# Feed-forward blocks in rounds of eight instead of steps of four: transposes, second layer and first layer grouped, with one bank for the first layer

## The reference, cut to what matters

```python
def _fff(x, node_w, node_b, w1, b1, w2, b2):
    for _ in range(DEPTH):                       # 4 levels, 15 nodes
        score = einsum('nd,nd->n', xf, node_w[cur]) + node_b[cur]
        cur = 2 * cur + 1 + (score >= 0)
    leaf = cur - N_NODES                         # one of 16 leaves
    hidden = relu(xf @ w1[leaf] + b1[leaf])      # 256 -> 64
    return hidden @ w2[leaf] + b2[leaf]          # 64 -> 256
q, k, v = _fff(x, q...), _fff(x, k...), _fff(x, v...)
attn = softmax(einsum('bqd,bkd->bqk', q, k) / 16)
return einsum('bqk,bkd->bqd', attn, v)
```

## Time and profile before

| | |
|---|---|
| median of 3 runs | 696.19 us (692.74 to 698.44) |
| span of the profiled execution | 651.9 us |
| median above that span | 44.3 us |
| TensorE busy | 585.3 us, 90% |
| VectorE busy | 439.3 us, 67% |
| ScalarE busy | 298.7 us, 46% |
| GpSimd busy | 236.6 us, 36% |
| FFN stage: transposes | 288, first at 429.8 us |
| FFN stage: last second-layer product starts | 554.1 us |

### The profile page before, as it was taken

The page is one execution under the profiler, slowest core; times in us unless marked ns, Lnnn a source line. Parts: engine busy times, 40 slices in busy tenths (PEclk is TensorE's granted clock), DMA queues, the critical chain, the costliest instruction groups (busy, mean ns, idle before and its releaser), DMA issues.

```text
span 651.9 us, 14814 instructions
## 1 busy us (share of the span) xinstructions
PE 585.3 (90%) x5131; PEld 492.2 (76%) x5131; DVE 439.3 (67%) x1511; ACT 298.7 (46%) x482; POOL 236.6 (36%) x298
## 2 busy tenths in 40 slices
PE   6577998999899999999999898769999999399996
PEld 6466787887787788878878776658888888289985
DVE  3755676888886888898888887845545553056664
ACT  4104444444443444544445454027777777133231
POOL 5700010053243243324323335740017777346431
PEclk9869999999998999999999999969999999599999
DMA  6898787898897999999888649969999999637552
GB/s 202 247 297 276 243 256 200 284 286 241 271 306 222 286 316 251 279 302 285 260 283 281 210 151 313 329 231 320 326 390 399 412 415 344 207 108 215 165 175 81
DMA packets 105015, 173.78 MB, mean 267 GB/s; under 512 B 14128, under 2 KB 73200, under 8 KB 104944
## 3 DMA queue, kind: packets, MB, share of 16 engines
q1 hardware_dynamic: 93088, 146.03, 70.7%
q0 software_dynamic: 9216, 25.18, 11.6%
q10 hardware_dynamic: 2640, 1.65, 0.9%
HBM read 92.59 MB, written 79.69 MB: 264 GB/s over the span
## 4 chain that ended last, share of the span: by engine, by line
PE 59%; DMA 14%; SPq 9%; DVE 8%; issue 4%; POOL 3%; ACT 2%; ACTq 1%; DVEq 0%; POOLq 0%
PE banks L524 7%; PE banks L567 5%; PE banks L807 5%; PE banks L818 5%; PE banks L833 5%; DMA parts_dram<-k_lo 5%; PE banks L875 5%; PE banks L539 4%; PE banks L551 4%; DMA parts_dram<-q_hi 3%; PE banks L896 3%; DVE mneg L1167 3%; PE banks L701 3%; SPq L330 3%; POOL k_all L1580 2%
## 5 line engine op out<-in xcount | busy, mean ns | idle before, releaser
L1167 DVE TENSOR_REDUCE mneg<-banks 128x2 f32<-128x512 f32 x240 | 121.8, 548 | 58.3 <-PE banks L540 58.3
L927 ACT ACTIVATE pt<-banks 128x768 f32<-128x768 f32 x128 | 103.4, 810 | 118.4 <-PE banks L552 118.3
L1521 POOL DMA_INDIRECT xs_dram<-xn2s,place x96 | 95.6, 996 | 163.6 <-ACT pt L927 128.8
L539 PE MATMUL banks<-k,q 107*128 107x256 f32 x240 | 76.8, 371 | 16.5 <-DVE mneg L1167 7.7
L551 PE MATMUL banks<-q,k 109*128 109x256 f32 x256 | 75.6, 347 | 1.0 <-ACT pt L927 0.4
L539 PEld LDWEIGHTS banks<-k,q 107*128 107x128 f32 x240 | 46.6, 194 | 24.4 <-DVE mneg L1167 11.4
L552 PE MATMUL banks<-q,k 109*128 109x128 f32 x256 | 57.3, 224 | 0.0
L567 PE MATMUL banks<-pt,vp 128*32 128x256 f32 (+1 forms) x1024 | 55.5, 335 | 0.4 <-ACT pt L927 0.4
L540 PE MATMUL banks<-k,q 107*128 107x128 f32 x240 | 54.4, 226 | 0.0
L1580 POOL DMA_INDIRECT q_all<-ys_dram,place x32 | 30.7, 960 | 62.7 <-DMA ys_dram<-yb 53.6
L551 PEld LDWEIGHTS banks<-q,k 109*128 109x128 f32 x256 | 48.8, 190 | 3.5 <-ACT pt L927 2.6
(11 more groups left out here) (177 smaller groups left out, 1293.9 us busy)
## 6 DMA issues: line engine op xcount, KB each, us to landing
ys_dram<-yb SPq DMA_DIRECT2D x36, 512.0 KB
xb<-xs_dram SPq DMA_DIRECT2D x35, 512.0 KB, 7.7
k<-parts_dram SPq DMA_DIRECT2D x128, 128.0 KB, 3.3
q<-parts_dram SPq DMA_DIRECT2D x128, 128.0 KB, 3.6
xs_dram<-zero SPq DMA_DIRECT2D x45, 256.0 KB
parts_dram<-q_hi SPq DMA_DIRECT2D x32, 256.0 KB, 3.7
xs_dram<-zero SPq DMA_DIRECT2D x18, 384.0 KB, 4.6
tables<-leafw SPq DMA_DIRECT2D x16, 257.0 KB
```

The lines of the kernel that those rows point to most:

```text
L539: mm(ps[:, 0:S], q[0:KN, t, P:S], k[0:KN, t, :], start=True, stop=True)
L927: nc.scalar.activation(pt[:, 2 * p:2 * p + 2, :], st_banks(b, p)[:, :, 0:S + P], ACT.Exp, scale=SC).then_inc(exp_sb, 1)
L1167: last = nc.vector.tensor_reduce(mneg[1 - u][:, t, 2 * j:2 * j + 2], S_BANKS[:, :, cols], axis=AX.X, op=ALU.max, negate=True)
L1521: gp.indirect_dma_start(xs_dram[tree], bass.IndirectOffsetOnAxis(ap=place[:, k:k + 1], axis=0), xn2s[m % RING][:, t, :], None).then_inc(sc ...
```

## The change

It regroups stage 2. A round handles two groups (eight blocks): transposes of groups q+4 and q+5, second layer of q and q+1, first layer of q+2 and q+3. ScalarE's list follows the same order. There are four tiles xbT instead of two, so the transposes run four groups ahead of the second layer. The even group is transposed into the banks 0 and 1, the odd one into 2 and 3. Both first layers of a round go side by side into the bank 3; so the second half of the odd group's transposes waits for the relus of the round before, and the first layer waits for the copies of the transposes in its own round. Each relu waits for the first layer of both groups. To make room for the larger xbT, the gathered q rows of the first 12 sequences lie in the space of the first tree's weight table (`wl0`). The layout within xbT is changed from (half, block, column) to (block, half, column), and the copy with it. SP's list is as it was; GpSimd's gathers differ only in where q goes.

```diff
+XT = 4
...
-        xbT = [sb(f"xbT{i}", [P, C, 4, P]) for i in range(2)]
+        xbT = [sb(f"xbT{i}", [P, 4, C, P]) for i in range(XT)]
...
+        H_BANK = banks[3]
...
             def block_T(q):
-                ge(pe, xbT_sb, q)
+                ge(pe, xbT_sb, q - 1)
                 for m in range(4):
...
+                    if q % 2 == 1 and m == 2:
+                        ge(pe, h_sb, 4 if q == 3 else 2 * (q - 3))
                     for c in range(C):
-                        last = nc.tensor.transpose(banks[c][:, m * P:m * P + P], xb[w][:, m, c * P:c * P + P], ident[:])
+                        first = (m % 2) * D + c * P
+                        last = nc.tensor.transpose(pairs[q % 2][:, m // 2, first:first + P], xb[w][:, m, c * P:c * P + P],
+                                                   ident[:])
...
             def block_h(q):
-                pe.wait_ge(xbT_sb, q + 1)
+                pe.wait_ge(xbT_sb, 2 if q < 2 else min(q - q % 2 + 4, Q))
...
-            block_T(0)
-            block_T(1)
-            block_h(0)
-            for q in range(Q):
-                if q + 2 < Q:
-                    block_T(q + 2)
-                if q + 1 < Q:
-                    block_h(q + 1)
-                block_out(q)
+            both(block_T, 0)
+            both(block_h, 0)
+            both(block_T, 2)
+            for q in range(0, Q, 2):
+                both(block_T, q + 4)
+                both(block_out, q)
+                both(block_h, q + 2)
...
             def copy_xT(q):
                 act.wait_ge(xbT_ps, q + 1)
-                ge(act, h_ps, q - 1)
+                ge(act, h_ps, q - XT + 1)
...
             def relu(q):
-                act.wait_ge(h_ps, q + 1)
+                act.wait_ge(h_ps, q - q % 2 + 2)
```

More of the change, by code:

```diff
@@ L62 @@
 QB = XB // 2
+XT = 4
+Q_IN_WL0 = 12
 AHEAD = 2
@@ L815, in block_h @@
                 for r in range(2):
+                    first = (q % 2) * D + r * P
                     for c in range(C):
                         for e in range(2):
-                            last = mm(banks[2 + q % 2][e * HID:(e + 1) * HID, r * P:r * P + P],
-                                      wb1[(2 * q + r) % UP][:, e, c * HID:c * HID + HID], xbT[q % 2][:, c, 2 * e + r, :],
+                            last = mm(H_BANK[e * HID:(e + 1) * HID, first:first + P],
+                                      wb1[(2 * q + r) % UP][:, e, c * HID:c * HID + HID], xbT[q % XT][:, 2 * e + r, c, :],
                                       start=(c == 0), stop=(c == C - 1))
@@ L839, in block_out, with both @@
                 last.then_inc(y_ps, 1)
[L841 to L849 removed]
+            def both(part, first):
+                for q in (first, first + 1):
+                    if q < Q:
+                        part(q)
+            both(block_T, 0)
[5 more added lines that the diff above has]
+                both(block_h, q + 2)
             pe.wait_ge(y_sb, Q)
@@ L859, in transposes @@
                     pe.wait_ge(k_late[b - KB], 16 * T)
-                for ps, src, done, free in ((banks[0], q_all, tq_ps, qT_sb), (banks[1], k_all, tk_ps, kT_sb)):
+                for ps, src, done, free in ((banks[0], q_rows_of(b), tq_ps, qT_sb), (banks[1], k_rows_of(b), tk_ps, kT_sb)):
                     ge(pe, free, b)
@@ L1019, in copy_xT @@
                 act.wait_ge(xbT_ps, q + 1)
-                ge(act, h_ps, q - 1)
-                nc.scalar.copy(xbT[q % 2][:].rearrange("p c m k -> p c (m k)"), pairs[0][:]).then_inc(xbT_sb, 1)
+                ge(act, h_ps, q - XT + 1)
+                nc.scalar.copy(xbT[q % XT][:].rearrange("p (a m) c k -> p a (m c k)", a=2), pairs[q % 2][:]).then_inc(xbT_sb, 1)
             def relu(q):
-                act.wait_ge(h_ps, q + 1)
+                act.wait_ge(h_ps, q - q % 2 + 2)
                 ge(act, y_ps, q - 1)
                 for r in range(2):
-                    nc.scalar.activation(hT[q % 2][:, r, :], banks[2 + q % 2][:, r * P:r * P + P], ACT.Relu,
+                    first = (q % 2) * D + r * P
+                    nc.scalar.activation(hT[q % 2][:, r, :], H_BANK[:, first:first + P], ACT.Relu,
                                          bias=wb2[(2 * q + r) % UP][:, D:D + 1]).then_inc(h_sb, 1)
@@ L1037, in _, with both @@
             Q = TREES * QUADB
[L1038 to L1046, removed]
+            def both(part, first):
+                for q in (first, first + 1):
+                    if q < Q:
+                        part(q)
+            both(copy_xT, 0)
+            both(relu, 0)
+            both(copy_xT, 2)
+            for q in range(0, Q, 2):
+                both(copy_xT, q + 4)
+                both(copy_y, q)
+                both(relu, q + 2)
             def copy_qT(i, u):
```

20 lines of the change are left out of this document (13 added, 7 removed).

## The result

The changed kernel takes **757.1 us** (median of 4 runs, 756.8 to 762.0), the kernel before beside it 696.0 (4 runs): a ratio of 1.087 [1.083, 1.092]. The forecast was 723.7, with 704 to 760. The direction held; the loss is 61 us where 27.5 were forecast. The tie between load and second layer that the prediction names is there, but on the chip of this result it is not the whole of the loss.

The account below looks back on a forecast made before the run. TensorE bound the FFN stage before; after, the loop of odd load and second layer. Stage 39 us longer, attention 30.5 late, 3 back: +27.5 on span 651.9 gives 679.4, plus 44.3 is 723.7 us, range 704 to 760.

Parts of the forecast that it names:

- The tie between load and second layer: FFN stage: an odd load follows the store one round before; rounds of 9.0 us against 6.7 of work.
- The shared bank and the relu wait: FFN stage: odd transposes wait for two relus, up to 0.2 us a round; 0.75 us twice in the last rounds.
- the bubbles: FFN stage: TensorE idle between kinds of matmul; at best half of 20.3 us goes, 10.2 us.
- rival a: FFN rounds: the clock falls in each new 2.3 us gap of TensorE; 36 us more, 759 us; chance 0.12.
- The size of L: Landing time of an odd load in the FFN stage: 5.1 us, the lowest measured with a store ahead.
- The tail: End of FFN stage: 13.3 us of TensorE work and relu waits after 580.1; attention starts near 594.6.
- the 3 us of clock given back: Start of attention: TensorE stands still 1 us, not 9.5, so first scores and transposes take 3 us less.
- The time around the span: Outside the profiled span: median 696.2 is 44.3 us above the span of 651.9; kept as it was.
- (b): FFN stage: landings of loads stay at 7.7 us; 39 us more, 763 us; chance 0.06.
- (c): FFN stage: landings of loads near 3.5 us; 15 x 1.6 us less, 700 us; chance 0.07.
- my own case: FFN stage: odd loads land in 5.1 us, within 4.4 to 6.5; 713 to 745 us; chance 0.70.
- (d): FFN stage: loads come in time, bubbles halve; 6.8 us faster, 689 us; decided at landing 2.8 us; chance 0.05.

Follow-up runs that it names:

- after_again: The changed kernel, no edit, run again on a chip where the kernel before takes 653.9 us: 721.9 us, 1.097.
- the two experiments that move 64 and 65 us by this tie alone: Kernel before with loads three steps nearer: 766.1 us, 1.093; changed kernel with loads six, not four, steps ahead: 656.5 us, 1.0045.
- after_late: The changed kernel with GpSimd's gathers of q and k held back until all second layers are done: 803.1 us, one run.
- after_ahead4: The changed kernel with each load issued behind store n-9 in place of n-7, a round earlier: 730.7 us, 1.045.
- ahead4_spread: The changed kernel with loads a round earlier and gather releases alternating between second layers and transposes: 709.0 us, 1.012.
- before_again: The kernel before, no edit, run for a second profile on the slower kind of chip: 700.0 us, span 697.9.
- after_loadfirst: The changed kernel with SP issuing the load ahead of the store, the tie kept: 692.0 us, 1.054.
- run 7: Not a run label: part of the words "One program can run 7% apart in two sessions"; no kernel or experiment has this name.
- ahead4_late: The changed kernel with loads a round earlier and gathers held back until all second layers are done: 741.1 us, one run.
- before_bursts: The kernel before with the gathers of two groups released at once: 701.7 us, 1.002.

## Why the prediction was right in kind and short in size

**Right.** The load of an odd group is tied to the second layer of the group two rounds earlier, one round between, and this sets the round. The places named for it appear in after_again: 16 waits of TensorE's transposes released by the load of xb (15 forecast: the 15 odd groups, and one even group with 1.0 us), 49.3 us in all, the idle DMA engines, SP's issues right behind the copy, and the two experiments that move 64 and 65 us by this tie alone. The shared bank and the relu wait cost nothing to speak of there (no transpose waits for a relu, and the two waits of 0.75 are 0.72 each), and the bubbles halve in rounds without a wait for a load (6.20 against 6.68 us). The start was right too: the second layer of group 0 began at 445.36 in after_again, forecast 445.1.

**Wrong, in sizes.** The sum against after_again, whose span is 720.8 where the same sum gives 679.4, 41.4 less:

- *The clock in the gaps* (rival a, given 0.12). The step that failed is "2.3 lies nearer the first": it compared one gap of 1.66 us and one of 4.84, took 2.3 as safe, and so put the clock at nothing in the sum. Eleven rounds have half clock, for two reasons that the text did not see: gaps of 2.3 and 2.7 us were not safe, and most gaps are longer than forecast (3.3 to 4.7 in nine rounds). A slow round costs 1.97 - 1.09 on the transposes, and the second layer to the copy takes up to 2.48 (519.35 to 521.82 is 2.47) where it takes 1.34 (485.10 to 486.44): up to 2.0 us a round, and 21 in all (9.8 on the transposes, 11.0 on the second layers up to the copy). Rival (a) priced a round at 2.4, near enough; its chance was what was wrong.
- *The size of L.* The step "so I take the lowest measured landing": 5.1 was forecast, 6.18 is the mean in the chain, 1.1 x 15 = 16 us. The value holds for a queue without gathers (5.32 in after_late), and the 5.1 itself is such a load: it was issued between 439 and 450 us, before any gather. The text said that the gathers "speak against less" and then priced them at nothing. The estimate from the Trainium skill (DMA: Bandwidth & Descriptors, Anatomy of one DMA), whose fit is for transfers that GpSimd issues while these come from SP, 4.0 us, is 2.2 below that mean; none in that chain was under 4.5.
- Both feed each other: a longer landing is a longer gap, and that a slower loop. Together the two give 37 us, measured are 36.2: 171.2 us from the second layer of group 0 (445.36) to that of group 30 (616.51), for the 135.0 of the sum.
- *The tail.* Attention starts 16.6 us after that second layer (633.12), forecast 14.5: 2.1 us. The last rows of k landed 6.25 us after their gather, forecast 5.79, and TensorE stood still for 2.89 us before attention where 1 was forecast. It was enough for the 3 us of clock given back not to come: from 633 to 636 us the granted clock is 0.50, and the first scores take 3.65 us for the forecast 1.73. The chain of after_again, to set beside the earlier trace rows:

```profile
626.74 6.25 DMA k_all<-ys_dram,place
...
633.12 1.95 PE banks L887 x8
...
635.93 3.65 PE banks L898 x8
```

0.3 (start) + 36.2 + 2.1 + 3.0 = 41.6 us, against the 41.4.

**Not in the prediction at all.** The account above is that of after_again. On the chip of the result, where the loss is 61 us, loosening the tie (after_ahead4) leaves 28.5 us. Spreading the releases of the gathers as well (ahead4_spread) leaves 8.4, in another session. The sum and its rivals have no term for stalls while gathers run; what makes these stalls, and why the changed order suffers more from them, stays open.

**Wrong, in the base.** "The time around the span" was put at 44.3 us. It is about 2: after_again has a span of 720.8 in an execution of 722.84, before_again 697.9 in 700.02. The 44 us were the difference between two kinds of chip, read as a constant. It happened to do little harm, because the loss is of like size on both (61 and 68 us); but the trace came from an execution without the stalls, and the times from a chip with them, and nothing in the sum could have shown a rival that lives on them.

**The other rivals.** (b), landings at 7.7, and (c), at 3.5, each had the wrong L: what came is my own case with 16 of (b)'s 39 us and 21 of (a)'s 36 on top. (d), faster, decided at a landing of 2.8; none came near it. Even with the tie gone the changed order gains nothing: 1.0045, for attention waits for the gathers, and these start 3.7 us later.

## What to carry to other kernels

When work is regrouped, count for each transfer how many groups lie between the event that allows its issue and its first use, before and after: a load that was hidden behind four steps of 3.3 us became the bound with one round. If the sum then has TensorE standing still for 2 us and more in each round, price the slow clock in a good part of the rounds, not in none (here eleven of 15, six of 15 in after_loadfirst), and take the landing from loads that share the engines with the same other traffic. Set a profile's span against its own execution's time before anything is added to it.

## What the runs showed of the hardware

- One program can run 7% apart in two sessions on two chips, steadily within each: 654 on two of the chips used and about 701 on two others, with medians within 2 us of each other in each pair. Each chip was used in one session, so chip and session are not told apart. On the slower kind, TensorE, ScalarE and VectorE stall while GpSimd issues gathers every 1.25 us (ScalarE for up to 17.6 us in after_ahead4, VectorE for up to 15.4 in before_again); with no gathers in the stage (after_late, ahead4_late) its rounds have no such stall. The cause is open. It depends on how the gathers meet the rest of the order (22 us off after_ahead4 when its releases alternate, across two sessions), but not simply on releases by twos (before_bursts).
- A store issued 0.36 us ahead of a load on the same queue makes the landing of that load (512 KB, the store's 512 KB ahead of it) longer by about 0.9 us (mean 6.18 against 5.27), and gathers on the same engines make it longer by as much (6.18 against 5.32 without them, on another chip; in after_again alone 6.65 behind the first gather against 5.33 ahead of it).
- After TensorE stood still for 1.09, 1.65 or 2.27 us in after_again its transposes ran at full clock (2.4 GHz), after 2.32 us and after every gap from 2.67 us on at half (1.2 GHz), and 2.52 us was between the two. In after_late one gap of 1.98 us was followed by half clock and one of 3.05 by full clock: the length of the gap alone does not decide it.
